# An LSTM's recurrent steps on one core: the weights as moving side, the state turned back each step

## The chip, the cores and the metric

The kernel runs on one core of a Trainium2 chip. The metric is the time of one execution in microseconds of device time. Three runs of the kernel before gave 6598.71, 6599.22 and 6603.01 us; the median is 6599.22.

## What is computed

Two layers on a batch of 64 graphs of 256 nodes with 256 features. The part that the change touches is the LSTM of the first layer, which reads the normalised output of the first graph stage:

```python
def _lstm(x, W_ih, W_hh, b_ih, b_hh):
    x_proj = jnp.einsum('btd,gd->btg', x, W_ih) + b_ih + b_hh
    ...
    def step(carry, xp):
        h, c = carry
        gates = xp + h @ W_hh.T
        i, f, g, o = jnp.split(gates, 4, axis=-1)
        c = jax.nn.sigmoid(f) * c + jax.nn.sigmoid(i) * jnp.tanh(g)
        h = jax.nn.sigmoid(o) * jnp.tanh(c)
        return ((h, c), h)
```

There are 64 sequences of 256 steps, 256 units and 4 x 256 gate values. Everything is float32. The rest (graph convolutions before and after, and a feed-forward layer with piecewise maxima) stays as it is.

## The kernel before

`full_kernel` runs six stages one after the other: `stage_gnn0`, `stage_lstm`, `stage_gnn1`, `stage_hinges`, `stage_tropical`, `stage_ffn`. All engines meet at a barrier between two stages. The tile `hx` [128, 2, 257, 64] lies in SBUF through the first three stages: partition and second index are the feature (or unit), the third is the step, the last is the sequence. `stage_gnn0` writes the inputs into places 1 to 256. `stage_lstm` reads the input of step t at place t+1 and later writes h of step t over it, so that `stage_gnn1` finds the states there.

In `stage_lstm` the gates lie with their units in the partitions and the sequences in the free dimension. Weights are the stationary side, 128x128 a call, and the state (128x64) or the input streams. One PSUM bank holds one gate of four steps (`ps_g[s][q]`, two sets s of four gates q). VectorE first writes the biases into a bank (`fill`, L505), then TensorE adds the input product of four steps at once (`input_part`, L567, 256 columns a call) and, step by step, the product of the state (L580, 64 columns a call, 16 calls a step). All matmuls are issued with `start=False`, onto the banks that were opened once at the start (L591). The gates are ordered g, i, f, o. In the steady state a step on TensorE is the state product of step t (L580) and the input product of one gate of the next group of four steps (L567); TensorE waits for `h_ready` before the first.

ScalarE takes tanh of g and sigmoid of i, f, o as each gate is done (L545), and tanh of c (L548). VectorE computes i*g (L512), c*f (L515), c (L518) and h (L521), which it writes straight into `hx`, and one fill a step (L505). GpSimd does nothing in this stage. Every engine runs the same steps; a semaphore count per step ties them together. Each float32 call of a matmul shows in the trace as two pairs of LDWEIGHTS (PEld) and MATMUL (PE), called passes below. A transpose is one pass.

Of the kernel before, what the change touches and what calls it, by code (L numbers as in the profile page):

```python
# [440 lines left out]
def stage_lstm(nc, a, hx):  # L441

    T, S = N, 4
    ROWS = GATES * H // P
    sems = []
    with ExitStack() as ctx:
# [34 lines left out]
        def _(sp):
            sp.dma_start(w_ih[:, :, :], a["w_ih_t"].rearrange("(k p) g -> p k g", p=P)).then_inc(const_in, 16)
            sp.dma_start(w_hh[:, :, :], a["w_hh_t"].rearrange("(k p) g -> p k g", p=P)).then_inc(const_in, 16)
            for e, name in enumerate(("b_ih", "b_hh")):
                sp.dma_start(bias[:, e, :, :], a[name].rearrange("m (q c) -> m q c", c=2)).then_inc(bias_in, 16)

        @block.vector
        def _(dve):  # L490
            dve.memset(hx[:, :, 0:1, :], 0.0).then_inc(zero_set, 1)
            dve.memset(c[:, :, :], 0.0).then_inc(zero_set, 1)
            dve.wait_ge(bias_in, 16 * 2)
            dve.tensor_tensor(bias_sum[:, :, :], bias[:, 0, :, :], bias[:, 1, :, :], ALU.add).then_inc(bias_ready, 1)
            dve.wait_ge(bias_ready, 1)
            for q in range(GATES):
                for c2 in range(2):
                    dve.tensor_copy(bias_wide[:, q, c2, :], bias_sum[:, q, c2:c2 + 1].to_broadcast([P, S * B]))\
                       .then_inc(bias_ready, 1)
            dve.wait_ge(bias_ready, 1 + 2 * GATES)  # L500
# [29 lines left out]
            for q in range(GATES):  # L530
                fill(0, q)
            groups(0)
            with dve.Fori(1, T // (2 * S)) as i:
                groups(i)

        @block.scalar
        def _(act):
            def step(t, s, r):
# [11 lines left out]
            def groups(i):  # L550
                for s in range(2):
                    for r in range(S):
                        step(2 * S * i + S * s + r, s, r)

            groups(0)
            with act.Fori(1, T // (2 * S)) as i:
                groups(i)

        @block.tensor
        def _(pe):  # L560
            def input_part(group, s, q):

                pe.wait_ge(bias_set, GATES * group + q + 1)
                for c2 in range(2):
                    row = (2 * q + c2) * P
                    for k in range(KD):
# [2178 lines left out]
```

## Time and profile before

| | |
|---|---|
| median of 3 runs | 6599.22 us |
| profiled execution | span 6600.3 us; no time beside its span is given for it |
| TensorE, matmul | 5873.0 us busy, 89% |
| TensorE, weight loads | 4098.8 us, 62% |
| VectorE | 5019.6 us, 76% |
| ScalarE | 3265.9 us, 49% |
| GpSimd | 1711.4 us, 26% |
| recurrent stage | from about 529 to 1915 us |

The spans are of one execution, counted from its first instruction. The shares are averages over six stages with different limits; the rows further down take the recurrent stage alone. PE is the matmul side of TensorE and PEld its weight loads, which run beside it; DVE is VectorE, ACT ScalarE, POOL GpSimd. Ends of matmuls are modelled in the trace, starts are measured.

### The profile page before, as it was taken

What the parts mean: (1) busy time and instruction counts of PE and PEld (TensorE: products, weight loads), DVE (VectorE), ACT (ScalarE), POOL (GpSimd) and SP (SyncE); (2) the same over time, 40 slices, a digit from 0 to 9 for tenths busy, and PEclk for the clock granted to TensorE, in tenths of its full rate; (3) what the DMA queues carried; (4) which work ended last, traced back from release to release, by engine and by line L of the source; (5) the groups of instructions that cost most, each with busy time, mean ns of one, the idle gap of its engine ahead of it and who ended that gap; (6) DMA issues with size and microseconds to landing.
All of it is one profiled execution on the core that took longest, in us unless ns stands there. A gap on an engine that the chain in (4) does not pass through costs nothing. (4 is left out here: it accounts for less than half of the span.)

```text
span 6600.3 us, 102260 instructions
## 1 busy us (share of the span) xinstructions
PE 5873.0 (89%) x29118; PEld 4098.8 (62%) x29118; DVE 5019.6 (76%) x9365; ACT 3265.9 (49%) x6025; POOL 1711.4 (26%) x3544
## 2 busy tenths in 40 slices
PE   9998999999988886399999999487676999999999
PEld 6667999999977775266666666354343444444444
DVE  8993333333348887799999999798686999999998
ACT  6662222222224443266666666121124777777777
POOL 3330000000004443266656655137561000000000
PEclk9999999999989998699999999799787999999999
DMA  4440000000014444122222222126453212222221
GB/s 135 135 137 21 0 0 0 0 0 0 0 45 153 153 153 141 60 72 72 73 75 72 72 75 73 33 101 217 160 203 109 83 64 83 77 74 72 83 83 45
DMA packets 359366, 528.00 MB, mean 80 GB/s; under 512 B 28208, under 2 KB 298160, under 8 KB 359248
## 3 DMA queue, kind: packets, MB, share of 16 engines
q1 hardware_dynamic: 322944, 400.58, 18.6%
q0 software_dynamic: 36304, 126.13, 5.6%
q8 instruction: 40, 0.66, 0.0%
q14 instruction: 78, 0.64, 0.0%
HBM read 297.48 MB, written 229.13 MB: 80 GB/s over the span
## 5 line engine op out<-in xcount | busy, mean ns | idle before, releaser
L1712 PE MATMUL t_fetched<-t_wpart,t_onehot 128*128 128x512 f32 x4096 | 1221.1, 420 | 36.1 <-DVE t_tout L1817 15.9
L1817 DVE SCALAR_TENSOR_TENSOR t_tout<-t_fetched,t_top,t_tout 128x1024 f32<-128x1024 f32 x896 | 1149.1, 1282 | 35.5 <-PE t_fetched L1712 4.5
L580 PEld LDWEIGHTS l_ps<-hx,l_whh 128*128 128x128 f32 x8192 | 962.5, 193 | 16.8 <-DVE hx L521 3.7
L580 PE MATMUL l_ps<-hx,l_whh 128*128 (+1 forms) x8192 | 950.5, 275 | 3.2 <-DVE hx L521 3.2
L1712 PEld LDWEIGHTS t_fetched<-t_wpart,t_onehot 128*128 128x128 f32 x4096 | 691.2, 188 | 269.0 <-DVE t_tout L1817 131.5
L545 ACT ACTIVATE l_act<-l_ps 128x128 f32<-128x128 f32 x1024 | 284.1, 278 | 1054.0 <-PE l_ps L580 1054.0
L2634 DVE SCALAR_TENSOR_TENSOR f_line<-f_hinge,f_vec,f_line 128x1024 f32<-128x1024 f32 x512 | 656.8, 1283 | 60.3 <-ACT f_hinge L2518 30.6
L2140 PE MATMUL ts_fetched<-t_wpart,ts_onehot 128*128 128x512 f32 x1608 | 509.5, 452 | 161.2 <-ACT ts_onehot L2115 71.3
L512 DVE TENSOR_TENSOR l_ig<-l_act 128x128 f32<-128x128 f32 x256 | 74.8, 292 | 592.1 <-ACT l_act L545 592.1
L2140 PEld LDWEIGHTS ts_fetched<-t_wpart,ts_onehot 128*128 128x128 f32 x1608 | 308.5, 209 | 309.9 <-DVE ts_tout L2208 196.2
L567 PE MATMUL l_ps<-hx,l_wih 128*128 (+1 forms) x2048 | 497.5, 386 | 1.0 <-DVE l_ps L505 1.0
L2555 PE MATMUL f_psc<-f_x,f_wc 128*128 128x512 f32 x1024 | 489.9, 601 | 0.0
L2568 PE MATMUL f_pso<-f_fused,f_wd 128*128 128x512 f32 x1024 | 463.0, 595 | 28.7 <-DVE f_fused L2621 28.7
L2555 PE MATMUL f_psg<-f_x,f_wg 128*128 128x512 f32 x1024 | 482.0, 593 | 0.0
L2112 ACT ACTIVATE ts_dist<-ts_index,t_pminus 128x256 f32<-128x256 f32 (+2 forms) x140 | 79.5, 568 | 655.0 <-PE ts_index L2131 544.6
L2518 ACT ACTIVATE f_hinge<-f_pst,f_vec 128x1024 f32<-128x1024 f32 x384 | 398.9, 1114 | 0.0
L567 PEld LDWEIGHTS l_ps<-hx,l_wih 128*128 128x128 f32 x2048 | 369.8, 190 | 41.5 <-issue 1.8
L2208 DVE SCALAR_TENSOR_TENSOR ts_tout<-ts_fetched,ts_top,ts_tout 128x1024 f32<-128x1024 f32 x296 | 380.0, 1284 | 13.4 <-PE ts_fetched L2140 3.0
L2568 PEld LDWEIGHTS f_pso<-f_fused,f_wd 128*128 128x128 f32 x1024 | 191.9, 190 | 283.6 <-issue 254.8
L775 POOL MEMSET g_half<- 128x2 f32 x1 | 0.1, 100 | 1395.5 <-POOLq L56 1395.5
L2555 PEld LDWEIGHTS f_psg<-f_x,f_wg 128*128 128x128 f32 x1024 | 195.6, 191 | 247.3 <-issue 247.3
L2525 ACT ACTIVATE f_spare<-f_pst,f_vec 128x1024 f32 x224 | 240.7, 1135 | 174.9 <-DVE f_pause L2659 174.9
(383 smaller groups left out, 10615.0 us busy)
## 6 DMA issues: line engine op xcount, KB each, us to landing
t<-t_tout SPq DMA_DIRECT2D x128, 512.0 KB, 2.6
f_t<-t SPq DMA_DIRECT2D x64, 1024.0 KB, 5.2
g_adj<-in_adj SPq DMA_DIRECT2D x128, 256.0 KB, 3.0
g_adjt<-in_adjt SPq DMA_DIRECT2D x128, 256.0 KB, 2.8
t_x<-x_normalised SPq DMA_DIRECT2D x130, 128.0 KB, 2.3
g_x<-in_x SPq DMA_DIRECT2D x64, 256.0 KB, 2.8
x_kept<-g_x SPq DMA_DIRECT2D x64, 256.0 KB, 2.2
g_x<-x_kept SPq DMA_DIRECT2D x64, 256.0 KB, 2.8
```

Source lines behind the costliest of these rows:

```text
L545: act.activation(act_g[q][:, :, :], ps_g[s][q][:, :, r, :], ACT.Tanh if q == 0 else ACT.Sigmoid)\
L567: pe.matmul(ps_g[s][q][:, c2, :, :], w_ih[:, k, row:row + P], hx[:, k, ds(S * group + 1, S), :], start=False, stop=False, skip_group_check ...
L580: mm = pe.matmul(ps_g[s][q][:, c2, r, :], w_hh[:, k, row:row + P], hx[:, k, ds(t, 1), :].rearrange("p o b -> p (o b)"), start=False, stop= ...
L1712: mm = pe.matmul(fetched[c % RING][:, h * CH:(h + 1) * CH], one_hot[g][:, c % GRP * P:(c % GRP + 1) * P], w_part[part][:, k, h * CH:(h + 1 ...
L1817: dve.scalar_tensor_tensor(t_out[j][:, :], column[:, :], value, t_out[j][:, :], ALU.add, ALU.max)\
L2140: mm = pe.matmul(fetched[buf][:, h * CH:(h + 1) * CH], one_hot[b][:, at * P:(at + 1) * P], w_part[part][:, half, h * CH:(h + 1) * CH], sta ...
L2208: dve.scalar_tensor_tensor(t_out[j][:, :], column[:, :], top[j][:, c:c + 1], (t_out if c else t_in)[j][:, :], ALU.add, ALU.max).then_inc(f ...
L2518: op = act.activation(hinge[v][:, k, :], ps_t[:, :], ACT.Relu, bias=column(u, "knot", k))
L2525: act.activation(spare[:, ds(k, 1), :].rearrange("p o t -> p (o t)"), ps_t[:, :], ACT.Relu, bias=column(u, "knot", k + SURE))
L2555: mm = pe.matmul(ps_[:, :], w_[:, k, u * P:(u + 1) * P], x[j][:, k, h * HB:(h + 1) * HB], start=(k == 0), stop=(k == KD - 1))
L2568: mm = pe.matmul(ps_o[k][:, h * HB:(h + 1) * HB], w_d[:, u, k * P:(k + 1) * P], fused[u % 2][:, h * HB:(h + 1) * HB], start=(u == 0), stop ...
L2634: dve.scalar_tensor_tensor(acc[:, :], source, column(u, "bend", k), acc[:, :], ALU.mult, ALU.add)\
```

## The change

The gates now lie with the sequences in the partitions: partitions 0 to 63 hold the 64 sequences for the first 128 units, 64 to 127 the same sequences for the other 128 units, and the free dimension holds the units of the gates. The stationary side of a matmul is the state or the input, [128, 64] (`h_t` or `x_now`), and the weights stream, 256 columns a call: one half of the units of two gates. The half c2 of the units is written at PSUM partitions 64*c2 and so uses columns 64*c2 to 64*c2+63 of the array. A pair p of gates (g and i, f and o) is done after 4 calls, both after 8 (L601). The input product is now made per step, one step ahead (8 calls), after the state product of the step. The bias fill is one copy of 512 elements a step as before.

h comes out of VectorE with the sequences in the partitions, so TensorE transposes it (L623, one call of 128x128 into `ps_ht`) and VectorE copies it from PSUM into one of two `h_t` tiles (L571), which is what the next step's state product waits for. GpSimd copies the state into `hx` (L531) and takes the next input out of `hx` into one of two `x_now` tiles (L522); before each copy it waits and does a one-element operation. The input product waits for `x_ready` and `bias_set`. ScalarE waits once for two gates. The banks are opened by 4 calls instead of 8. The loops are unrolled by 4 steps instead of 8. On the host the biases are laid out by halves.

```diff
-    T, S = N, 4
-    ROWS = GATES * H // P
+    T, U = N, 4
+    AHEAD = 1
+    HB = B
+    PAIRS = GATES // 2
...
-        w_ih = sb("l_wih", [P, KD, GATES * H])
-        w_hh = sb("l_whh", [P, KD, GATES * H])
-        bias = sb("l_bias", [P, 2, GATES, 2])
-        bias_sum = sb("l_bias_sum", [P, GATES, 2])
-        bias_wide = sb("l_bias_wide", [P, GATES, 2, S * B])
-        act_g = [sb(f"l_act{q}", [P, 2, B]) for q in range(GATES)]
-        c = sb("l_c", [P, 2, B])
-        ig = sb("l_ig", [P, 2, B])
-        tc_ = sb("l_tc", [P, 2, B])
-        ps_g = [[ctx.enter_context(nc.psum_tensor(f"l_ps{s}{q}", [P, 2, S, B], F32)) for q in range(GATES)]
-                for s in range(2)]
+        w_ih = sb("l_wih", [P, KD, GATES, 2, P])
+        w_hh = sb("l_whh", [P, KD, GATES, 2, P])
+        bias = sb("l_bias", [P, 2, GATES, P])
+        bias_sum = sb("l_bias_sum", [P, GATES, P])
+        act_g = [sb(f"l_act{q}", [P, P]) for q in range(GATES)]
+        c = sb("l_c", [P, P])
+        ig = sb("l_ig", [P, P])
+        tc_ = sb("l_tc", [P, P])
+        h = sb("l_h", [P, P])
+        ident = sb("l_ident", [P, P])
+        h_t = [sb(f"l_ht{j}", [P, KD, HB]) for j in range(2)]
+        x_now = [sb(f"l_x{j}", [P, KD, HB]) for j in range(2)]
+        pool_pause, pool_zero = sb("l_pool_pause", [1, 4]), sb("l_pool_zero", [1, 1])
+        ps_g = [ctx.enter_context(nc.psum_tensor(f"l_ps{j}", [P, PAIRS, 512], F32)) for j in range(2)]
+        ps_ht = ctx.enter_context(nc.psum_tensor("l_psht", [P, KD, HB], F32))
...
+        def groups(eng, step):
+            for r in range(U):
+                step(r, r)
+            with eng.Fori(1, T // U - 1) as i:
+                for r in range(U):
+                    step(U * i + r, r)
+            for r in range(U):
+                step(T - U + r, r)
...
+        @block.gpsimd
+        def _(pool):
+            def held(k, sem_, value):
+                pool.wait_ge(sem_, value)
+                pool.tensor_tensor(pool_pause[:, k:k + 1], pool_zero[:, :], pool_zero[:, :], ALU.add)
+            def take_x(t, j):
+                pool.tensor_copy(x_now[j][:, :, :], hx[:, :, ds(t + 1, 1), :].rearrange("p k o b -> p k (o b)"))\
+                    .then_inc(x_ready, 1)
+            def step(t, r):
+                if within(t, AHEAD + 1):
+                    held(r % 2, x_used, t + AHEAD)
+                    take_x(t + AHEAD + 1, (r + AHEAD + 1) % 2)
+                held(2 + r % 2, h_t_ready, t + 1)
+                pool.tensor_copy(hx[:, :, ds(t + 1, 1), :].rearrange("p k o b -> p k (o b)"), h_t[r % 2][:, :, :])\
+                    .then_inc(h_kept, 1)
+            pool.memset(pool_zero[:, :], 0.0).then_inc(pool_zero_set, 1)
+            pool.wait_ge(pool_zero_set, 1)
+            take_x(0, 0)
+            take_x(1, 1)
+            groups(pool, step)
...
-            def fill(s, q):
-                dve.tensor_copy(ps_g[s][q][:, :, :, :].rearrange("p c r b -> p c (r b)"), bias_wide[:, q, :, :])\
-                   .then_inc(bias_set, 1)
-            def step(t, s, r):
-                fill(1 - s, r)
+            def fill(r):
+                dve.tensor_copy(ps_g[r % 2][:, :, 0:2 * P], bias_sum[:, :, :].rearrange("p (o q) u -> p o (q u)", q=2))                   .then_inc(bias_set, 1)
+            def step(t, r):
+                if within(t, AHEAD):
+                    fill(r + AHEAD)
                 dve.wait_ge(act_ready[0], t + 1)
                 dve.wait_ge(act_ready[1], t + 1)
-                dve.tensor_tensor(ig[:, :, :], act_g[0][:, :, :], act_g[1][:, :, :], ALU.mult).then_inc(ig_ready, 1)
+                dve.tensor_tensor(ig[:, :], act_g[0][:, :], act_g[1][:, :], ALU.mult).then_inc(ig_ready, 1)
                 dve.wait_ge(act_ready[2], t + 1)
                 wait_past(dve, c_ready, t)
-                dve.tensor_tensor(c[:, :, :], c[:, :, :], act_g[2][:, :, :], ALU.mult).then_inc(fc_ready, 1)
+                dve.tensor_tensor(c[:, :], c[:, :], act_g[2][:, :], ALU.mult).then_inc(fc_ready, 1)
                 dve.wait_ge(ig_ready, t + 1)
                 dve.wait_ge(fc_ready, t + 1)
-                dve.tensor_tensor(c[:, :, :], c[:, :, :], ig[:, :, :], ALU.add).then_inc(c_ready, 1)
+                dve.tensor_tensor(c[:, :], c[:, :], ig[:, :], ALU.add).then_inc(c_ready, 1)
                 dve.wait_ge(act_ready[3], t + 1)
                 dve.wait_ge(tanh_c_ready, t + 1)
-                dve.tensor_tensor(hx[:, :, ds(t + 1, 1), :].rearrange("p k o b -> p k (o b)"), act_g[3][:, :, :],
-                                  tc_[:, :, :], ALU.mult).then_inc(h_ready, 1)
-            def groups(i):
-                for s in range(2):
-                    for r in range(S):
-                        step(2 * S * i + S * s + r, s, r)
+                dve.tensor_tensor(h[:, :], act_g[3][:, :], tc_[:, :], ALU.mult).then_inc(h_ready, 1)
+                dve.wait_ge(h_turned, t + 1)
+                wait_past(dve, h_kept, t - 1)
+                dve.tensor_copy(h_t[r % 2][:, :, :], ps_ht[:, :, :]).then_inc(h_t_ready, 1)
...
+            def step(t, r):
                 for q in range(GATES):
-                    act.wait_ge(gate_done[q], t + 1)
-                    if q == 0:
-                        wait_past(act, h_ready, t)
-                    act.activation(act_g[q][:, :, :], ps_g[s][q][:, :, r, :], ACT.Tanh if q == 0 else ACT.Sigmoid)\
+                    if q % 2 == 0:
+                        act.wait_ge(pair_done[q // 2], t + 1)
+                    act.activation(act_g[q][:, :], ps_g[r % 2][:, q // 2, (q % 2) * P:(q % 2 + 1) * P], ACT.Tanh if q == 0 else ACT.Sigmoid)\
                        .then_inc(act_ready[q], 1)
                 act.wait_ge(c_ready, t + 1)
-                act.activation(tc_[:, :, :], c[:, :, :], ACT.Tanh).then_inc(tanh_c_ready, 1)
...
+            def half(j, c2, p):
+                return ps_g[j][c2 * HB:(c2 + 1) * HB, p, 0:2 * P].rearrange("b (q u) -> b q u", u=P)
+            def products(p, j, source, w, last):
+                for k in range(KD):
+                    for c2 in range(2):
+                        mm = pe.matmul(half(j, c2, p), source[:, k, :], w[:, k, 2 * p:2 * p + 2, c2, :],
+                                       start=False, stop=last and k == KD - 1, skip_group_check=True)
+                return mm
+            def input_part(t, j):
+                pe.wait_ge(x_ready, t + 1)
+                pe.wait_ge(bias_set, t + 1)
+                for p in range(PAIRS):
+                    mm = products(p, j, x_now[j], w_ih, False)
+                mm.then_inc(x_used, 1)
+            def step(t, r):
+                wait_past(pe, h_t_ready, t)
+                for p in range(PAIRS):
+                    products(p, r % 2, h_t[(r + 1) % 2], w_hh, True).then_inc(pair_done[p], 1)
+                if within(t, AHEAD):
+                    input_part(t + AHEAD, (r + AHEAD) % 2)
+                pe.wait_ge(h_ready, t + 1)
+                pe.transpose(ps_ht[:, :, :].rearrange("p k b -> p (k b)"), h[:, :], ident[:, :]).then_inc(h_turned, 1)
+            pe.wait_ge(const_in, 16 * 3)
+            for j in range(2):
+                for p in range(PAIRS):
+                    mm = pe.matmul(ps_g[j][:, p, :], ident[:, :], w_ih[:, 0, :, 0, :], start=True, stop=True)
             mm.then_inc(banks_opened, 1)
             pe.wait_ge(zero_set, 2)
-            for q in range(GATES):
-                input_part(0, 0, q)
-            for s in range(2):
-                steps(0, s, False)
-            with pe.Fori(1, T // (2 * S) - 1) as i:
-                for s in range(2):
-                    steps(i, s, False)
-            for s in range(2):
-                steps(T // (2 * S) - 1, s, s == 1)
+            for r in range(AHEAD):
+                input_part(r, r)
+            groups(pe, step)
```

TensorE, in the loop, one step before (`l_ps00` is set 0, gate 0; L580 is the state product, L567 the input product, counts are calls):

```order
L580 MATMUL l_ps00<-hx,l_whh 128x64 [waits l_h_ready]
L580 MATMUL l_ps00<-hx,l_whh 128x64 x3
L580 MATMUL l_ps01<-hx,l_whh 128x64 x4
L580 MATMUL l_ps02<-hx,l_whh 128x64 x4
L580 MATMUL l_ps03<-hx,l_whh 128x64 x4
L567 MATMUL l_ps13<-hx,l_wih 128x256 [waits l_bias_set]
L567 MATMUL l_ps13<-hx,l_wih 128x256 x3
```

The same engine and place now (`l_ht` is the turned state, `l_x` the input, `l_psht` the transpose of h):

```order
L601 MATMUL l_ps1<-l_whh,l_ht0 64x256 [waits l_h_t_ready]
L601 MATMUL l_ps1<-l_whh,l_ht0 64x256 x7
L607 REGISTER_ALU
L601 MATMUL l_ps0<-l_wih,l_x0 64x256 [waits l_bias_set,l_x_ready]
L601 MATMUL l_ps0<-l_wih,l_x0 64x256 x7
L623 MATMUL l_psht<-l_ident,l_h 128x128 [waits l_h_ready]
```

The 16 calls on 128x128 weights and 4 of the input product have become 8 and 8 with a 128x64 stationary side, and a step ends with a transpose that waits for h; the next state product waits for the copy of it.

VectorE in the loop, one step before (L505 is the fill, L521 writes h):

```order
L510 REGISTER_ALU
L512 TENSOR_TENSOR l_ig<-l_act0,l_act1 128x128 [waits l_act_ready1,l_act_ready0]
L515 TENSOR_TENSOR l_c<-l_c,l_act2 128x128 [waits l_c_ready,l_act_ready2]
L518 TENSOR_TENSOR l_c<-l_c,l_ig 128x128 [waits l_fc_ready,l_ig_ready]
L521 ISA [waits l_tanh_c_ready,l_act_ready3]
L521 TENSOR_TENSOR hx<-l_act3,l_tc 128x2x64
L505 COPY l_ps03<-l_bias_wide 128x512
```

VectorE now (L551 is the fill, L567 writes h, L571 copies the transpose):

```order
L556 REGISTER_ALU
L558 TENSOR_TENSOR l_ig<-l_act0,l_act1 128x128 [waits l_act_ready1,l_act_ready0]
L561 TENSOR_TENSOR l_c<-l_c,l_act2 128x128 [waits l_c_ready,l_act_ready2]
L564 TENSOR_TENSOR l_c<-l_c,l_ig 128x128 [waits l_fc_ready,l_ig_ready]
L567 TENSOR_TENSOR l_h<-l_act3,l_tc 128x128 [waits l_tanh_c_ready,l_act_ready3]
L571 COPY l_ht0<-l_psht 128x128 [waits l_h_kept,l_h_turned]
L551 COPY l_ps0<-l_bias_sum 128x2x256
```

The register instruction ahead of h is gone and a copy out of PSUM that waits for `h_turned` and `h_kept` has come in; the fill of the next step stands behind it.

GpSimd now, one step of the loop; it had no instruction here before:

```order
L518 TENSOR_TENSOR l_pool_pause<-l_pool_zero 1x1 [waits l_x_used]
L522 ISA
L522 COPY l_x1<-hx 128x128
L518 TENSOR_TENSOR l_pool_pause<-l_pool_zero 1x1 [waits l_h_t_ready]
L531 ISA
L531 COPY hx<-l_ht1 128x2x64
L518 TENSOR_TENSOR l_pool_pause<-l_pool_zero 1x1 [waits l_x_used]
```

The copy of an input and the copy of a state alternate, each behind a wait and a pause of one element.

## Rows read from the trace of the kernel before

**Rows 1.** Windows: us, then busy us and count of PE, PEld, DVE, ACT, POOL, granted clock.
```profile
552.00:1915.00 1363.00, 1358.83 (x10211) 1306.08 (x10209) 455.62 (x1279) 336.31 (x1281) 0.00 (x0) 0.99 0.00 0
...
1899.00:1907.00 8.00, 6.93 (x33) 6.74 (x33) 1.61 (x6) 1.31 (x5) 0.00 (x0) 0.50 0.01 2
```

**Rows 2.** Waits from 600 to 1900 us: who waited for whom, total, times, longest.
```profile
ACT l_act L545 <- PE l_ps L580: 978.7, 980, 2.1
...
PE l_ps L580 <- DVE hx L521: 2.1, 2, 1.1
```

**Rows 3.** Timeline of one step in the loop: start us, duration us, engine, line, operation.
```profile
1400.31 3.68 PE L580 MATMUL l_ps<-hx,l_whh 128*128 x32
...
1403.13 0.28 ACT L545 ACTIVATE l_act<-l_ps 128x128 f32<-128x128 f32 x1 [0.62 <-PE l_ps L580]
1403.44 0.29 DVE L515 TENSOR_TENSOR l_c<-l_c,l_act 128x128 f32<-128x128 f32 x1 [0.53 <-ACT l_act L545]
...
1403.82 1.95 PE L567 MATMUL l_ps<-hx,l_wih 128*128 x8
1403.84 0.29 DVE L518 TENSOR_TENSOR l_c<-l_c,l_ig 128x128 f32<-128x128 f32 x1
1404.02 0.28 ACT L545 ACTIVATE l_act<-l_ps 128x128 f32<-128x128 f32 x1 [0.62 <-PE l_ps L580]
1404.20 0.30 ACT L548 ACTIVATE l_tc<-l_c 128x128 f32<-128x128 f32 x1
1404.71 0.29 DVE L521 TENSOR_TENSOR hx<-l_act,l_tc 128x128 f32 x1 [0.58 <-ACT l_tc L548]
...
1405.61 0.33 PE L580 MATMUL l_ps<-hx,l_whh 128*128 x2
```

**Rows 4.** Timeline of a step outside the loop.
```profile
561.50 0.30 ACT L548 ACTIVATE l_tc<-l_c 128x128 f32<-128x128 f32 x1
561.90 0.29 DVE L521 TENSOR_TENSOR hx<-l_act,l_tc 128x128 f32<-128x128 f32 x1 [0.47 <-ACT l_tc L548]
```

**Rows 5.** Timeline of the stage's start: the banks opened, the first input product; durations min/median/max.
```profile
534.66 9.68 PE L591 MATMUL l_ps<-hx,l_wih 128*128 128x512 f32 x16 [11.54 <-DMA l_whh<-in_w_hh_t]
...
542.46 0.19 PEld L591 LDWEIGHTS l_ps<-hx,l_wih 128*128 128x128 f32 x1 [0.24 <-issue]
...
545.33 7.14 PE L567 MATMUL l_ps<-hx,l_wih 128*128 128x256 f32 x32 [0.98 <-DVE l_ps L505]
...
L580 PEld LDWEIGHTS l_ps<-hx,l_whh x8192: 186/192/338, 552.1 to 1913.5; 128*128 128x128 f32 x200
...
L567 PE MATMUL l_ps<-hx,l_wih x2048: 379/379/454, 545.3 to 1887.7; 128*128 x175, 128*128 128x256 f32 x12
```

**Rows 6.** Timeline of the last steps, without an input product.
```profile
1887.91 3.68 PE L580 MATMUL l_ps<-hx,l_whh 128*128 128x64 f32 x32
...
1888.94 0.28 ACT L545 ACTIVATE l_act<-l_ps 128x128 f32<-128x128 f32 x1 [2.14 <-PE l_ps L580]
...
1892.65 5.06 PE L580 MATMUL l_ps<-hx,l_whh 128*128 128x64 f32 x32 [1.07 <-DVE hx L521]
1893.80 0.28 ACT L545 ACTIVATE l_act<-l_ps 128x128 f32<-128x128 f32 x1 [1.70 <-PE l_ps L580]
...
1914.75 0.29 DVE L521 TENSOR_TENSOR hx<-l_act,l_tc 128x128 f32 x1 [1.39 <-ACT l_tc L548]
```

**Rows 7.** Timeline of the next stage: four transposes in a stream, and four after a wait.
```profile
2209.67 0.60 PE L875 MATMUL g_ps_xn3t<-g_ident,g_xn 128*128 128x128 f32 x4
...
2209.69 0.99 DVE L964 TENSOR_SCALAR g_xn<-g_x,g_mv,g_rstd 128x256 f32<-128x256 f32 x2 [0.86 <-POOL g_rstd L788]
...
2210.74 0.66 PE L875 MATMUL g_ps_t<-g_ident,g_xn 128*128 128x128 f32 x4 [0.47 <-DVE g_xn L964]
```

**Rows 8.** GpSimd's groups of this size: count, busy us, mean ns.
```profile
L1615 POOL TENSOR_TENSOR t_poolpause<-t_logshare 1x1 f32<-1x1 f32 x384 | 70.3, 183 | 513.2 <-DVE t_done L1826 510.4 <-DVE t_cand L1805 2.8
L793 POOL TENSOR_TENSOR g_adjt<-g_adjt,g_ident 128x128 f32<-128x128 f32 x128 | 58.8, 480 | 0.0
```

More of the change, by code:

```diff
@@ L482, in _, with within @@
+        def within(t, ahead):
+            return not isinstance(t, int) or t + ahead < T
         @block.sync
         def _(sp):
-            sp.dma_start(w_ih[:, :, :], a["w_ih_t"].rearrange("(k p) g -> p k g", p=P)).then_inc(const_in, 16)
-            sp.dma_start(w_hh[:, :, :], a["w_hh_t"].rearrange("(k p) g -> p k g", p=P)).then_inc(const_in, 16)
+            for w, name in ((w_ih, "w_ih_t"), (w_hh, "w_hh_t")):
+                sp.dma_start(w[:, :, :, :, :].rearrange("p k q c u -> p k (q c u)"),
+                             a[name].rearrange("(k p) g -> p k g", p=P)).then_inc(const_in, 16)
+            sp.dma_start(ident[:, :], a["ident"]).then_inc(const_in, 16)
@@ L489, in _ @@
         @block.vector
         def _(dve):
-            dve.memset(hx[:, :, 0:1, :], 0.0).then_inc(zero_set, 1)
-            dve.memset(c[:, :, :], 0.0).then_inc(zero_set, 1)
-            dve.wait_ge(bias_in, 16 * 2)
+            dve.memset(h_t[1][:, :, :], 0.0).then_inc(zero_set, 1)
+            dve.memset(c[:, :], 0.0).then_inc(zero_set, 1)
+            dve.wait_ge(bias_in, 16 * 4)
             dve.tensor_tensor(bias_sum[:, :, :], bias[:, 0, :, :], bias[:, 1, :, :], ALU.add).then_inc(bias_ready, 1)
@@ L495, in _ @@
             dve.wait_ge(bias_ready, 1)
-            for q in range(GATES):
[L497 to L500, printed above, removed]
-            dve.wait_ge(zero_set, 2)
-            def fill(s, q):
-                dve.tensor_copy(ps_g[s][q][:, :, :, :].rearrange("p c r b -> p c (r b)"), bias_wide[:, q, :, :])\
-                   .then_inc(bias_set, 1)
@@ L530, in _ @@
[L530 to L534, printed above, removed]
+                dve.tensor_tensor(h[:, :], act_g[3][:, :], tc_[:, :], ALU.mult).then_inc(h_ready, 1)
+                dve.wait_ge(h_turned, t + 1)
+                wait_past(dve, h_kept, t - 1)
+                dve.tensor_copy(h_t[r % 2][:, :, :], ps_ht[:, :, :]).then_inc(h_t_ready, 1)
+            dve.wait_ge(banks_opened, 1)
+            for r in range(AHEAD):
+                fill(r)
@@ L546, in step @@
                        .then_inc(act_ready[q], 1)
                 act.wait_ge(c_ready, t + 1)
-                act.activation(tc_[:, :, :], c[:, :, :], ACT.Tanh).then_inc(tanh_c_ready, 1)
-            def groups(i):
-                for s in range(2):
[L552 to L557, printed above, removed]
+                act.activation(tc_[:, :], c[:, :], ACT.Tanh).then_inc(tanh_c_ready, 1)
@@ L559, in _ @@
+            groups(act, step)
         @block.tensor
         def _(pe):
[L561 to L566, printed above, removed]
-                        pe.matmul(ps_g[s][q][:, c2, :, :], w_ih[:, k, row:row + P],
-                                  hx[:, k, ds(S * group + 1, S), :], start=False, stop=False,
-                                  skip_group_check=True)
@@ L571, in steps @@
-            def steps(i, s, last):
-                group = 2 * i + s
-                for r in range(S):
-                    t = S * group + r
-                    wait_past(pe, h_ready, t)
-                    for q in range(GATES):
-                        for c2 in range(2):
-                            row = (2 * q + c2) * P
-                            for k in range(KD):
-                                mm = pe.matmul(ps_g[s][q][:, c2, r, :], w_hh[:, k, row:row + P],
-                                               hx[:, k, ds(t, 1), :].rearrange("p o b -> p (o b)"), start=False,
-                                               stop=(r == S - 1 and c2 == 1 and k == KD - 1), skip_group_check=True)
-                        mm.then_inc(gate_done[q], 1)
-                    if not last:
-                        input_part(group + 1, 1 - s, r)
@@ L588, in _ @@
-            pe.wait_ge(const_in, 16 * 2)
-            for s in range(2):
-                for q in range(GATES):
-                    mm = pe.matmul(ps_g[s][q][:, :, :, :], w_ih[:, 0, 0:P], hx[:, 0, ds(1, 2 * S), :], start=True, stop=True)
+            def half(j, c2, p):
+                return ps_g[j][c2 * HB:(c2 + 1) * HB, p, 0:2 * P].rearrange("b (q u) -> b q u", u=P)
+            def products(p, j, source, w, last):
+                for k in range(KD):
+                    for c2 in range(2):
+                        mm = pe.matmul(half(j, c2, p), source[:, k, :], w[:, k, 2 * p:2 * p + 2, c2, :],
+                                       start=False, stop=last and k == KD - 1, skip_group_check=True)
+                return mm
@@ L601, in _ @@
-            for s in range(2):
-                steps(T // (2 * S) - 1, s, s == 1)
+            for r in range(AHEAD):
+                input_part(r, r)
+            groups(pe, step)
     clear_semaphores(nc, sems)
@@ L2706, in columns, with by_half @@
         return np.ascontiguousarray(v.reshape(-1, P).T)
+    def by_half(v):
+        return np.ascontiguousarray(v.reshape(GATES, 2, P).transpose(1, 0, 2).reshape(2, -1))
     ones = np.ones((P, P), np.float32)
@@ L2715 @@
         "w_hh_t": turned(gates_first_g(given["L0_ffn_W_hh"])),
-        "b_ih": columns(gates_first_g(given["L0_ffn_b_ih"])), "b_hh": columns(gates_first_g(given["L0_ffn_b_hh"])),
+        "b_ih": by_half(gates_first_g(given["L0_ffn_b_ih"])), "b_hh": by_half(gates_first_g(given["L0_ffn_b_hh"])),
         "w_lin_t": turned(given["L0_ffn_W_lin"]), "b_lin": given["L0_ffn_b_lin"].reshape(1, 2),
```

14 lines of the change are left out of this document (7 added, 7 removed).

## The prediction

> **What bounds the kernel now.** I read the windows by stage first: of 6600.3 us the recurrent stage (552 to 1915) holds 1363, and in it TensorE is busy for 1358.8 while VectorE has 456, ScalarE 336 and GpSimd nothing [rows 1]. The waits say the same from the other side: 980 waits of ScalarE for TensorE, and only two of TensorE for the new state [rows 2]. The timeline of one step shows why. A step begins with 32 passes of the state's product (two per call, 16 calls), 3.51 us from 1400.31 to 1403.82, then 8 passes of the input's product, 1.79 us; the next step's first pass is at 1405.61, so a step is 5.30 us of TensorE alone [rows 3]. The state was ready at 1405.00, 0.6 us before it could be used. In the product of the state each pass streams only 64 columns but loads 128x128 weights, and costs 0.110 us; a pass of 256 columns costs (7.14 - 0.38) / 31 = 0.218 us [rows 5]. So the loads of weights set the pace in two thirds of the step, and that is what the change goes for.
>
> **The change, part by part.**
>
> *The products.* State and input become the stationary side (128x64) and the weights stream, 256 columns at a time. Each product is now 8 calls, 16 passes: 4 pairs, one call of each pair for each half of the array's columns. One behind the other they are 16 x 0.218 = 3.49 us. If a pass on one half runs beside a pass on the other, the order of the calls (both passes of one half, both of the other) lets the second pass of each call run beside the first of the next: 9 slots of 0.218 where a product stands alone, 1.96 us; both products of a step behind each other take 17 slots, 3.71 us, instead of 5.30. No row of this kernel has a stationary side of 64 columns, so the trace bounds it from both sides: 3.71 and 32 x 0.218 = 6.98 us. I take 3.71: the passes use different cells and write different partitions, and the rows show that TensorE already does two things at once, loads of 0.192 us beside passes that follow each other every 0.110 us [rows 3, 5]. The Trainium skill (TensorEngine Tiling (Array Packing), Key Properties) says that different tiles can execute loads and matmuls in parallel; no run here shows it. By it the step's products are the 3.71, without it the 6.98.
>
> *The chain.* With that TensorE no longer covers the chain of one step, so it has to be added up. From the first pass of the state's product: the last starts 8 slots later, 1.74; it takes 0.38 [rows 5]; 0.03 to ScalarE, and the sigmoid of f is 0.28; 0.03 and 0.29 for c*f; 0.11 and 0.29 for the add; 0.07 and 0.30 for the tanh [rows 3]; 0.10 and 0.29 for h, the distance that the steps outside the loop show (561.80 to 561.90) [rows 4]. In the loop it is 0.21 because the address of hx goes through a register, which now falls to GpSimd. That is 3.91. New behind it: TensorE takes up work 0.06 after the write it waits for (2210.68 to 2210.74); one transpose from idle is 0.33, by the four that take 0.66 after a wait and start 0.11 apart [rows 7]; 0.10 (two waits) and 0.29 for VectorE's copy out of PSUM, by its other operations of this size; 0.06 to TensorE, and 0.12 for a first pass whose weights could not be loaded ahead: after a wait the first activation came 1.15 us after the first pass (1892.65 to 1893.80), else 1.03 (1887.91 to 1888.94) [rows 6]. Sum: **4.87 us** against 5.30.
>
> *Does TensorE keep up?* 3.71 of products and 0.16 until the last has left the array end at 3.87, just before the transpose can start at 3.97. If TensorE sets the end instead, the step is 3.71 + 0.16 + 0.33 + 0.10 + 0.29 + 0.06 + 0.12 = 4.77. The two are 0.10 apart: whatever lengthens the products by more than that is paid in full. The switch between half and full tiles twice a step has no row. Its bounds are 0 and one emptying of the array, 0.16; I take 0, since the array is empty at both switches by this sum. The Trainium skill (same page and section) asks that the engine be drained at such a switch; by it nothing changes while these waits stand.
>
> *GpSimd* gets two pauses (0.18) and two copies of 128x128 a step (0.48 for a two-input operation of this size) [rows 8]: 1.3 us of 4.87. Its copy of the input is due one product of the state later, its copy of h two steps later; neither ends last. VectorE has 5 operations of 0.29 and the fill of 0.69: 2.1 us, and the fill lies under the state's product.
>
> *Ends.* Opening the banks takes 8 passes of 512 instead of 16: 3.4 us less at 0.43 (0.19 and 0.24) a pass [rows 5]. The first input product takes 1.74 instead of 6.98. So the first step starts 8.6 us sooner. Before, the steps run from 552.31 (545.33 + 6.98) to the end of the last h at 1915.04, 1362.7 us [rows 5, 6]; now 255 x 4.87 + 5.4 (copy and last write by GpSimd) = 1247.3. Together 115.4 + 8.6 = **124 us less**. The page gives the profiled execution by its span, 6600.3, which is 1.1 us above the median of the three runs, 6599.2; taken from the median it gives **6475**. Every 0.01 us a step is 2.6 us; the step that changes nothing is 5.35.
>
> **Rivals.**
> - *Loads of the second half come late* (slower). This is the mechanism that decides the sign. While one pass runs on each half, the next weights for half A stand in the queue behind a pass for half B that has to wait. If they can't be taken past it, each call starts later by one load of 64 columns, half of the 0.110 that a load of 128 costs where loads set the pace [rows 3]: 0.055. A step's TensorE bound becomes 4.77 + 16 x 0.055 = 5.65, and the time 6475 + 256 x 0.78 = 6675. It decides from 0.036 us a call. For it: this interleaving of half tiles appears nowhere in the trace. Against it: loads do run beside passes on full tiles. The Trainium skill (TensorE: Matmul & The Clock Gate, Part 3, The mechanism) says that a load overlaps a running matmul only when the rows of the array differ; both halves here use all rows, so by that rule this rival, or worse, holds. The rows of the state's product disagree for full tiles.
> - *The halves don't run side by side*: the change does not do what it says. 6.98 + 1.06 = 8.04 us a step, 7286 us. Nothing in the trace excludes it.
> - *The clock falls.* The granted clock was 0.99 over the stage and 0.50 (1.2 of 2.4 GHz) in its last steps, when the input's product was gone and TensorE waited 1.07 us a step for the state [rows 1, 6]. Passes then took twice as long. The new step has gaps too (0.1 and 0.5 us). If it fell for good, 3.71, 0.16 and 0.33 double: 4.77 + 4.20 = 8.97 us, 7525. Against it: the gaps are half as long and the products fill three quarters of the step.
>
> **How the numbers follow.** Forecast 0.47, with its own range of 6431 (0.17 less a step: 0.03 instead of 0.07 before the tanh and 0.10 before the copy, half the 0.12) to 6544 (0.11 more for register waits, 0.16 for a switch). Late loads 0.33, of which 0.08 below the deciding 0.036. Serial halves 0.14, low clock 0.06. The predicted time is the first case's. The range takes in the first two, 0.80: 6430 to 6700, the top at 0.061 us a call. A measurement of this kernel tells 0.2%, 13 us, from no change. Faster 0.47 + 0.08 = 0.55, same 0.04 (steps of 5.30 to 5.40), slower 0.41.
>
> **What would show it.** Right: h to h of 4.8 to 5.0 us; passes of L601 starting in near pairs, 16 of them in about 2 us; TensorE waiting for h before each transpose and for h_t before each state product; clock 1.00. Late loads: starts of the calls 0.25 or more apart, and the transpose starting when the input's product ends while h is long there. Serial: 16 passes in 3.5 us. Wrong in the chain: a tail from the last pass to the first of the next step other than 2.75 us. Stages before and after should keep their lengths.

## The result, and the profile after

The changed kernel takes **6392.94 us** (median of four runs, 6392.48 to 6393.44) against 6599.88 us of the kernel before beside it (6598.71 to 6603.01): ratio 0.9684, 95% interval 0.967 to 0.9698, 207 us less. The forecast was 6475, range 6430 to 6700. The sign is as forecast, and so is what was to bring it, the two halves side by side; the time is 37 us below the range.

The stage by windows (us, then busy us and count of PE, PEld, DVE, ACT, POOL, granted clock), the answer to [rows 1]:

```profile
552.00:1700.00 1148.00, 1015.00 (x8367) 595.29 (x8367) 528.94 (x1524) 304.96 (x1270) 199.80 (x1012) 1.00 0.00 0
1690.00:1700.00 10.00, 6.77 (x53) 3.68 (x51) 4.03 (x13) 2.40 (x10) 0.82 (x4) 1.00 0.00 0
```

TensorE is no longer busy all the time (1015 of 1148 us, before 1358.8 of 1363), and its clock stays at 1.00, that is 2.4 GHz, in the last steps too, where it was 0.50 before. The waits from 600 to 1900 us (total, times, longest) answer to [rows 2]:

```profile
ACT l_act L584 <- PE l_ps L601: 664.2, 487, 2.4
...
PEld l_ps L601 <- DVE l_ht L571: 144.8, 243, 0.7
...
PEld l_psht L623 <- DVE l_h L567: 139.3, 244, 2.3
```

Two waits of the product for the state have become one a step, and the transpose has its own: the chain of the step now sets the pace. One step in the loop, and the copy of the step ahead (start, duration), the answer to [rows 3]:

```profile
999.54 0.29 DVE L571 COPY l_ht<-l_psht 128x128 f32<-128x128 f32 x1 [0.51 <-PE l_psht L623]
...
1004.04 0.29 DVE L571 COPY l_ht<-l_psht 128x128 f32<-128x128 f32 x1 [0.42 <-PE l_psht L623]
...
1004.38 1.49 PEld L601 LDWEIGHTS l_ps<-l_whh,l_ht 128*64 128x64 f32 x16 [0.57 <-DVE l_ht L571]
1004.38 1.95 PE L601 MATMUL l_ps<-l_whh,l_ht 128*64 128x256 f32 x16 [0.38 <-DVE l_ht L571]
...
1005.51 0.45 ACT L584 ACTIVATE l_act<-l_ps 128x128 f32<-128x128 f32 x2 [2.29 <-PE l_ps L601]
...
1006.16 1.90 PE L601 MATMUL l_ps<-l_wih,l_x 128*64 128x256 f32 x16
1006.38 0.45 ACT L584 ACTIVATE l_act<-l_ps 128x128 f32<-128x128 f32 x2 [0.42 <-PE l_ps L601]
1006.69 0.29 DVE L561 TENSOR_TENSOR l_c<-l_c,l_act 128x128 f32<-128x128 f32 x1 [0.33 <-ACT l_act L584]
1007.08 0.29 DVE L564 TENSOR_TENSOR l_c<-l_c,l_ig 128x128 f32<-128x128 f32 x1
1007.41 0.31 ACT L587 ACTIVATE l_tc<-l_c 128x128 f32<-128x128 f32 x1 [0.58 <-DVE l_c L564]
1007.82 0.29 DVE L567 TENSOR_TENSOR l_h<-l_act,l_tc 128x128 f32<-128x128 f32 x1 [0.44 <-ACT l_tc L587]
...
1008.17 0.33 PE L623 MATMUL l_psht<-l_ident,l_h 128*128 128x128 f32 x1
1008.53 0.29 DVE L571 COPY l_ht<-l_psht 128x128 f32<-128x128 f32 x1 [0.42 <-PE l_psht L623]
...
1008.88 0.63 PEld L601 LDWEIGHTS l_ps<-l_whh,l_ht 128*64 128x64 f32 x8 [0.57 <-DVE l_ht L571]
```

From the first pass at 1004.38 to the next step's at 1008.88 it is 4.50 us. The input's product begins 1.78 after the state's, so 16 passes take 8 slots. The transpose starts 0.35 after h, the copy 0.36 later, the next product 0.35 after that; from tanh to h it is 0.41, against 0.40 in [rows 4]. The sigmoid of f stands in the second ACT row of two operations (1006.38), 2.00 after the first pass. Of the steps in the loop, which is unrolled by four, every fourth is 0.09 longer: VectorE's copy comes 0.45 after the transpose's start and not 0.36 (it stood for 0.51 us at 999.54, for 0.42 at 1004.04); in that step VectorE has a register instruction of 0.04 us ahead of the copy (999.46), for the count of `h_kept`, which itself waits for the transpose; in the others it has none there. The mean over the stage is 4.517 us, from GpSimd's first copy of a state (548.3) to its last (1700.1), 255 steps. The start of the stage answers to the timeline in [rows 5]:

```profile
534.28 5.64 PE L628 MATMUL l_ps<-l_wih,l_ident 128*128 128x512 f32 x8 [12.01 <-DMA l_ident<-in_ident]
...
540.90 1.95 PE L601 MATMUL l_ps<-l_wih,l_x 128*64 128x256 f32 x16 [0.98 <-DVE l_ps L551]
...
542.65 1.93 PE L601 MATMUL l_ps<-l_whh,l_ht 128*64 128x256 f32 x16
```

The groups (count, busy us, mean ns, idle before) and durations of single tiles (min/median/max ns) answer to the durations in [rows 5] and to [rows 7, 8]:

```profile
L601 PE MATMUL l_ps<-l_whh,l_ht 128*64 128x256 f32 x4096 | 498.5, 385 | 103.2 <-DVE l_ht L571 103.2
...
L531 POOL COPY hx<-l_ht 128x128 f32 (+1 forms) x256 | 71.6, 280 | 0.0
```

```profile
L623 PE MATMUL l_psht<-l_ident,l_h x256: 327/328/329, 547.4 to 1699.3; 128*128 128x128 f32 x128
L571 DVE COPY l_ht<-l_psht x256: 291/292/292, 547.8 to 1699.6; 128x128 f32<-128x128 f32 x128
```

GpSimd's copies take 280 ns, not the 480 of the two-input operation that stood in for them, and end long before anyone needs them.

### The profile page after: what moved, and what is told of

Its sections match the earlier page's. It is cut to its first block and busy times, and to the rows that moved or that the text cites. A ratio compares the mean times of both kernels' runs of the same rounds, so it can differ in the third digit from the quotient of the medians.

```text
span 6390.7 us, 100252 instructions
## 1 busy us (share of the span) xinstructions
PE 5520.0 (86%) x27318; PEld 3377.2 (53%) x27318; DVE 5095.3 (80%) x9609; ACT 3238.1 (51%) x6025; POOL 1914.4 (30%) x4567
## 5 line engine op out<-in xcount | busy, mean ns | idle before, releaser
L584 ACT ACTIVATE l_act<-l_ps 128x128 f32<-128x128 f32 x1024 | 228.2, 275 | 716.9 <-PE l_ps L601 716.9
L601 PE MATMUL l_ps<-l_whh,l_ht 128*64 128x256 f32 x4096 | 498.5, 385 | 103.2 <-DVE l_ht L571 103.2
L601 PE MATMUL l_ps<-l_wih,l_x 128*64 128x256 f32 x4096 | 485.6, 379 | 1.0 <-DVE l_ps L551 1.0
L601 PEld LDWEIGHTS l_ps<-l_whh,l_ht 128*64 128x64 f32 x4096 | 271.7, 136 | 262.6 <-DVE l_ht L571 151.9
L518 POOL TENSOR_TENSOR l_pool_pause<-l_pool_zero 1x1 f32<-1x1 f32 x510 | 93.8, 184 | 972.0 <-DVE l_ht L571 956.1
L601 PEld LDWEIGHTS l_ps<-l_wih,l_x 128*64 128x64 f32 x4096 | 294.7, 137 | 148.9 <-issue 1.8
L2665 DVE SCALAR_TENSOR_TENSOR f_line<-f_spare,f_vec,f_line 128x1024 f32<-128x1024 f32 x224 | 287.8, 1285 | 44.2 <-DVE f_line L2665 44.2
```

The source lines that it names most:

```text
L518: pool.tensor_tensor(pool_pause[:, k:k + 1], pool_zero[:, :], pool_zero[:, :], ALU.add)
L584: act.activation(act_g[q][:, :], ps_g[r % 2][:, q // 2, (q % 2) * P:(q % 2 + 1) * P], ACT.Tanh if q == 0 else ACT.Sigmoid)\
L601: mm = pe.matmul(half(j, c2, p), source[:, k, :], w[:, k, 2 * p:2 * p + 2, c2, :], start=False, stop=last and k == KD - 1, skip_group_chec ...
L2665: dve.scalar_tensor_tensor(acc[:, :], source, column(u, "bend", k), acc[:, :], ALU.mult, ALU.add)\
```

## The experiments

The steps are means: from the first to the last copy of a state by GpSimd, over 255, and for the kernel before 1362.7 / 256.

| | us | ratio to before, 95% | step, us |
|---|---|---|---|
| before | 6599.88 | | 5.32 |
| changed | 6392.94 | 0.9684 [0.967, 0.9698] | 4.517 |
| e1_one_half | 7235.24 | 1.096 [1.0928, 1.0991] | 7.778 |
| e2_halves_grouped | 6400.23 | 0.9695 [0.9667, 0.9723] | 4.556 |
| e3_not_turned | 7289.25 | 1.1041 [1.1009, 1.1074] | 3.794 |
| e4_input_one_call | 6527.62 | 0.9888 [0.9859, 0.9916] | 5.332 |
| e5_f_before_o | 6354.96 | 0.9621 [0.9605, 0.9637] | 4.358 |
| e6_split_and_late | 6289.27 | 0.952 [0.9504, 0.9536] | 4.100 |

The kernel before took 6600.51 beside e1 to e4 and 6606.54 beside e5 and e6.

### e1: all calls on one half of the array

```diff
-                return ps_g[j][c2 * HB:(c2 + 1) * HB, p, 0:2 * P].rearrange("b (q u) -> b q u", u=P)
+                return ps_g[j][0:HB, p, 0:2 * P].rearrange("b (q u) -> b q u", u=P)
```

> All calls of both products write to partitions 0 to 63, so none has a neighbour on the other half of the array; the gates of the other 64 partitions are left out (they keep the bias). Theory A, passes on the two halves run side by side: without a neighbour the 32 passes of a step come every 0.215 us, 6.9 us, and with 0.33 for the transpose, 0.04 + 0.29 for the copy and 0.05 + 0.05 to the next product a step is 7.6 to 7.8 us instead of 4.49, about 7200 us. Theory B, a pass with a stationary side of 64 columns is by itself twice as fast, whichever half it is on: passes every 0.107 us as before, a step of 4.49, 6393 us.

Measured 7235.24, a step of 7.78. From its timeline:

```profile
1000.88 0.29 DVE L567 TENSOR_TENSOR l_h<-l_act,l_tc 128x128 f32<-128x128 f32 x1 [0.45 <-ACT l_tc L587]
...
1002.78 0.33 PE L623 MATMUL l_psht<-l_ident,l_h 128*128 128x128 f32 x1
...
1003.49 3.67 PE L601 MATMUL l_ps<-l_whh,l_ht 128*64 128x256 f32 x16 [0.38 <-DVE l_ht L571]
...
1007.00 2.32 PE L601 MATMUL l_ps<-l_wih,l_x 128*64 128x256 f32 x10
```

The state's 16 passes take 3.51 us until the input's begin (1003.49 to 1007.00), almost twice the 1.78 of the changed kernel, and the transpose stands 1.9 us behind h, until the products are through. The streams, loads and counts are the same in both; only the place in the array differs. So the two halves do run side by side, and it is this that carries the change: with streamed weights alone a step would be 2.46 us longer than before. The Trainium skill (TensorEngine Tiling (Array Packing), Key Properties) says that tiles load and multiply in parallel; this run agrees for the matmuls, at a factor of 3.51 / 1.78 = 1.97.

### e2: each half's four passes one behind the other

```diff
-                for k in range(KD):
-                    for c2 in range(2):
+                for c2 in range(2):
+                    for k in range(KD):
```

> The same calls, those of one half of the units behind one another (both k of half 0, then both k of half 1, for each pair of gates). Theory A with strict order: in each group of four passes three have no neighbour, 25 slots of 0.215 for the two products instead of 16, 5.4 us, a step of about 6.1 us, 6800 us. Theory A where a pass may start ahead of others that wait for the other half, four or more ahead: nothing changes, 4.49 and 6393 us. Theory B: nothing changes either.

Measured 6400.23, 7 us more than the changed kernel (the intervals of the two ratios overlap) and 0.04 a step by the traces. In program order four passes of one half now come ahead of the first of the other. If passes started in that order, each group of four would share only one slot with the next, 13 slots or 2.8 us a product. Windows of 0.02 to 0.03 us of PE at the product's start show how many passes run (the count in brackets), first e2, then the changed kernel, then e1:

```profile
1002.30:1002.32 0.02, 0.02 (x2) 1.00 0.00 0
```

```profile
1004.38:1004.40 0.02, 0.02 (x2) 1.00 0.00 0
```

```profile
1003.49:1003.52 0.03, 0.03 (x1) 1.00 0.00 0
```

Two passes run from the first moment where there are two halves, even where the second half's first pass is the fifth in the queue, and one where there is one half. A pass that waits for its half does not hold back passes of the other. That is the reason why a product takes 8 slots and not 9. Late loads do show in this run, at a small price: for the second pair of gates the load of the second half starts only with the first half's pass (1003.22), and from the next passes on the two halves start 0.06 apart (1003.43 and 1003.49) instead of 0.01. The 0.04 a step can come from there; nothing was tried on it. The Trainium skill (TensorE: Matmul & The Clock Gate, Part 3, The mechanism) lets a load run beside a matmul only if their rows differ; both halves here use all rows, and their loads are hidden all the same (16 loads between 1004.38 and 1005.87, under passes with a pair every 0.215 us), so the measurement decides.

### e3: the state not turned back

```diff
-                dve.tensor_tensor(h[:, :], act_g[3][:, :], tc_[:, :], ALU.mult).then_inc(h_ready, 1)
-                dve.wait_ge(h_turned, t + 1)
                 wait_past(dve, h_kept, t - 1)
-                dve.tensor_copy(h_t[r % 2][:, :, :], ps_ht[:, :, :]).then_inc(h_t_ready, 1)
+                dve.tensor_tensor(h_t[r % 2][:, :, :].rearrange("p k b -> p (k b)"), act_g[3][:, :], tc_[:, :], ALU.mult)\
+                   .then_inc(h_t_ready, 1)
...
-                pe.wait_ge(h_ready, t + 1)
-                pe.transpose(ps_ht[:, :, :].rearrange("p k b -> p (k b)"), h[:, :], ident[:, :]).then_inc(h_turned, 1)
```

> The turning back of the state is left out: VectorE writes h as it lies into the tile that the next product reads, without transpose and copy (so the recurrence is another one). If the chain through h sets the step, the 0.37 of the transpose and 0.34 of the copy go: 4.49 - 0.71 = 3.78 us a step, 182 us less, about 6211 us. If TensorE's own work set the step (32 passes, 3.44, plus 0.05), the gain would end at about 3.5 to 3.8 as well, so it is told by whether the product waits for the state. Rival: the step is set by something else (GpSimd's copies), then little changes.

The step is 3.794 us, 0.72 less. The total, 7289.25, says nothing of that: the stages with piecewise maxima do work that depends on the values they get, and these are others here. The groups of lines show far more of a loop (`tg_fetched`, 2048 passes) that takes 64 passes in the changed kernel, and more rounds of another (1736 passes against 1608):

```profile
L2322 PE MATMUL tg_fetched<-t_wpart,tg_runrows 128*128 128x512 f32 x2048 | 678.7, 483 | 403.0 <-DVE tg_runrows L2339 264.5 <-DVE tg_acc L2356 138.5
...
L2167 PE MATMUL ts_fetched<-t_wpart,ts_onehot 128*128 128x512 f32 x1736 | 544.0, 446 | 175.1 <-DVE ts_tout L2235 76.4 <-ACT ts_onehot L2142 61.8 <-issue 20.3
```

So of this run only the recurrent stage is read. Turning costs the chain what the timeline of the changed kernel shows, 0.35 and 0.36 us; 0.01 is left. A price of the switch between half and full tiles would stand inside these links and the next: the transpose starts 0.06 after h ends and the product 0.06 after the copy ends, and here, where the array never leaves its halves, the product starts 0.05 after h ends (1004.44 + 0.29 to 1004.78). So a switch of an idle array costs 0.01 at most. TensorE did both products of a step every 3.79 us here.

### e4: seven of eight calls of the input product left out

```diff
-                for p in range(PAIRS):
-                    mm = products(p, j, x_now[j], w_ih, False)
+                mm = pe.matmul(half(j, 1, 0), x_now[j][:, 0, :], w_ih[:, 0, 0:2, 1, :],
+                               start=False, stop=False, skip_group_check=True)
```

> Of the input product of each step one call of eight is left; seven are left out. Theory A of the cover: the input product lies wholly under the chain, so a step stays at 4.49 and the time at 6393 as long as the clock stays. The clock is the question: before, it fell in the last steps when the input product was gone. If it falls here too, the state product doubles to 3.4 and the transpose slows, 4.49 + 1.56 + 0.3 = 6.3 to 6.6 us a step, 6860 to 6930 us. I expect the fall.

The step is 5.33 us, *longer* than with the input product. The data of later stages differ here too (1464 passes of the same loop), so the step counts. The clock over the stage, and two products of the state:

```profile
600.00:1900.00 1300.00, 899.03 (x4626) 455.80 (x4628) 506.83 (x1460) 291.54 (x1215) 191.63 (x972) 0.78 0.00 0
```

```profile
999.58 1.95 PE L601 MATMUL l_ps<-l_whh,l_ht 128*64 128x256 f32 x16 [0.38 <-DVE l_ht L571]
...
1003.37 0.33 PE L623 MATMUL l_psht<-l_ident,l_h 128*128 128x128 f32 x1 [1.41 <-DVE l_h L567]
...
1004.08 3.56 PE L601 MATMUL l_ps<-l_whh,l_ht 128*64 128x256 f32 x16 [0.38 <-DVE l_ht L571]
...
1009.47 0.33 PE L623 MATMUL l_psht<-l_ident,l_h 128*128 128x128 f32 x1 [1.33 <-DVE l_h L567]
```

The first product runs at 2.4 GHz (1.95 us) and its step is 4.50 (999.58 to 1004.08), just that of the changed kernel: the input product costs the chain nothing. The next takes 3.56 us for the same 16 passes, at 1.2 GHz, and from transpose to transpose it is 6.10 us. The clock did not stay down, as I had expected, but went in and out, 0.78 on the mean. What TensorE did otherwise is in the rows: it stood idle for 1.3 to 1.4 us before each transpose, where in the changed kernel the input product ran. So the input product, free by itself, also keeps the clock up; less work for TensorE made a longer step.

### e5: f ahead of o

Each set of gates gets three banks (g and i; f; o), filled by two copies instead of one, and f and o are made by calls of 128 columns, so that f is done before o.

```diff
+            def products(p, j, source, w, last, qs=(0, 1)):
+                lo, n = qs[0], len(qs)
+                if p == 1 and n == 2:
+                    products(1, j, source, w, last, (0,))
+                    return products(1, j, source, w, last, (1,))
...
-                for p in range(PAIRS):
-                    products(p, r % 2, h_t[(r + 1) % 2], w_hh, True).then_inc(pair_done[p], 1)
+                products(0, r % 2, h_t[(r + 1) % 2], w_hh, True).then_inc(pair_done[0], 1)
+                products(1, r % 2, h_t[(r + 1) % 2], w_hh, True, (0,)).then_inc(pair_done[1], 1)
+                products(1, r % 2, h_t[(r + 1) % 2], w_hh, True, (1,)).then_inc(o_done, 1)
```

> f and o are no pair any more: f is computed by calls of 128 columns ahead of o, each in a bank of its own (three banks a set), in both products; the fill is two copies; nothing is left out. Theory S, a pass costs what its columns stream: a call of 128 columns half a slot (0.107), so f is done 0.43 us sooner. The chain would be 4.06 us, but TensorE's own work (3.44 for both products, then 0.05, 0.06, 0.37, 0.34 and the copy's wait) holds a step at 4.2 to 4.35: 6330 to 6355 us. Theory L, weight loads set a floor of 0.107 us a pass: 48 passes are 5.1 us, a step 5.9 us, 6750 us.

Measured 6354.96, a step of 4.358. One step of it:

```profile
1002.27 1.72 PEld L605 LDWEIGHTS l_ps<-l_whh,l_ht 128*64 128x64 f32 x24 [0.66 <-DVE l_ht L573]
1002.28 1.96 PE L605 MATMUL l_ps<-l_whh,l_ht 128*64 128x256 f32 x24 [0.47 <-DVE l_ht L573]
...
1003.41 0.71 ACT L588 ACTIVATE l_act<-l_ps 128x128 f32<-128x128 f32 x3 [2.64 <-PE l_ps L605]
...
1004.06 1.91 PE L605 MATMUL l_ps<-l_wih,l_x 128*64 128x256 f32 x24
1004.16 0.28 DVE L563 TENSOR_TENSOR l_c<-l_c,l_act 128x128 f32<-128x128 f32 x1
...
1005.29 0.29 DVE L569 TENSOR_TENSOR l_h<-l_act,l_tc 128x128 f32<-128x128 f32 x1 [0.45 <-ACT l_tc L591]
...
1005.90 0.33 PE L629 MATMUL l_psht<-l_ident,l_h 128*128 128x128 f32 x1
...
1006.61 1.96 PE L605 MATMUL l_ps<-l_whh,l_ht 128*64 128x256 f32 x24 [0.39 <-DVE l_ht L573]
```

24 passes, 8 of them of 256 columns and 16 of 128, take 1.78 us (1002.28 to 1004.06), as 16 of 256 did: on halves a pass of 128 columns costs half of one of 256, and the loads set no floor at twice their rate. c*f starts 1.88 after the first pass instead of 2.31. But the transpose comes 0.61 after h and not 0.35: now the input product ends last, and more than half of what f gave is paid there. 0.10 of it comes with the change to a full tile behind running passes: the last pair of the input product starts at 1005.69 and the transpose 0.21 later, where pairs of 128 columns follow each other every 0.11; its load starts only there too (1005.90), so the two are not told apart. (0.43 less 0.26 is 0.17; the mean step fell by 0.16.)

### e6: and the last quarter of the input product behind the transpose

```diff
                 pe.transpose(ps_ht[:, :, :].rearrange("p k b -> p (k b)"), h[:, :], ident[:, :]).then_inc(h_turned, 1)
+                if within(t, AHEAD):
+                    input_rest((r + AHEAD) % 2)
```

On top of e5: `input_part` makes g, i and f, and `input_rest` makes o.

> As e5_f_before_o, and the last quarter of the input product (that of o) is issued behind the transpose, where TensorE waits for the copy. Theory S: TensorE no longer holds the transpose up, and the chain alone sets the step: 4.49 - 0.43 = 4.06 us, 110 us less than the changed kernel, 6283 us. Theory L: 5.3 us a step, 6600 us.

Measured 6289.27 (6286.12 to 6291.99), a step of 4.100. Its ratio to the kernel before, 0.952, lies clear of the changed kernel's 0.9684: it beats both, by 317 us and, with the difference of the ratios, 108 us. The place that mattered:

```profile
1005.29 0.29 DVE L569 TENSOR_TENSOR l_h<-l_act,l_tc 128x128 f32<-128x128 f32 x1 [0.45 <-ACT l_tc L591]
...
1005.64 0.33 PE L634 MATMUL l_psht<-l_ident,l_h 128*128 128x128 f32 x1
...
1005.90 0.66 PE L605 MATMUL l_ps<-l_wih,l_x 128*64 128x128 f32 x8
1006.01 0.29 DVE L573 COPY l_ht<-l_psht 128x128 f32<-128x128 f32 x1 [0.42 <-PE l_psht L634]
...
1006.39 1.92 PE L605 MATMUL l_ps<-l_whh,l_ht 128*64 128x256 f32 x24
```

The transpose is back at 0.35 behind h, and o's passes fill the time of VectorE's copy (1005.90 to the next product at 1006.39), which costs 0.03 at that end: 0.38 from copy to product instead of 0.35. The first of them starts 0.26 after the transpose, where full-tile transposes follow each other every 0.11 [rows 7]: a switch behind a running pass is not free here either, but the copy covers it.

## Why the forecast was right in kind and wrong in size

**The step.** I had 4.87 us; it is 4.50 in most steps and 4.517 on the mean. 255 x 0.353 is 90 us, somewhat more than the whole miss of the span, 86 (forecast 6600.3 - 124.0 = 6476.3, measured 6390.7). By my own terms:

| term | forecast | measured |
|---|---|---|
| first pass to the last | 8 slots, 1.74 | 1.78 less one slot of 0.22: 1.56 |
| first pass whose weights are not there | 0.12 more | in the 1.56 |
| last pass, and to the sigmoid of f | 0.38 + 0.03 | 0.44 |
| f to c*f, to the add | 0.31, 0.40 | 0.31, 0.39 |
| add to tanh | 0.29 + 0.07 | 0.33 |
| tanh to h | 0.30 + 0.10 | 0.41 |
| h to transpose | 0.29 + 0.06 | 0.35 |
| transpose to copy | 0.33 + 0.10 | 0.36 |
| copy to product | 0.29 + 0.06 | 0.35 |
| sum | 4.87 | 4.50 |

- *The step of the forecast that failed* is the first: "9 slots of 0.218 where a product stands alone", with the last pass 8 slots after the first, and 0.12 for weights "that could not be loaded ahead". It held passes to their order in the program. The halves fill at once (two passes in the first 0.02 us; e2), so the last pair starts after 7 slots. The 0.12 was misread from [rows 6]. In the step at 1892.65, after a wait, the second pass comes 0.160 after the first and the others 0.112 apart, so the first costs 0.05 more; the step at 1887.91, which I compared it with, is itself short at its start, its second pass comes 0.055 after the first. Here the second pair comes 0.267 after the first instead of 0.216, 0.05 again. Slot and misreading together are 0.30 of the 0.37 between 4.87 and 4.50.
- *The links* to the tanh and to the copy were 0.03 and 0.07 shorter than I took them; for the copy I had put "two waits" at 0.10, and the 0.07 ahead of the tanh was read in a step where ScalarE was still at the sigmoid of o (1404.02 + 0.28, the tanh at 1404.20) [rows 3]. Both lay in my low end. They count 256 times: 26 us.
- My low end, 6431, allowed 0.17 less a step, with half of the 0.12 in it but no slot: the order of the passes, which I had assumed and no row showed, should have been bounded from both sides as the other unknowns were.
- *TensorE's own bound* of 4.77 was too high as well: in e5, where the input product ends last, a step is 4.33 us (1002.28 to 1006.61).
- *The signs named.* h to h of 4.8 to 5.0 us: it was 4.50. 16 passes in about 2 us, in near pairs: 1.78, in pairs. TensorE waiting for h and for h_t, clock 1.00: so it was. A tail other than 2.75 us was to mean that the chain was wrong: from the end of the last pass (1005.94 + 0.38) to 1008.88 it is 2.56, the 0.12 and the 0.07 less.

**Ends.** The banks took 8 passes as forecast, and the first step starts 9.7 us sooner (552.31 to 542.65), against 8.6. The steps end 6.0 us after 255 mean steps, against 5.4. So the stage, from 542.65 to 1700.41, is 1157.8 us against my 1247.3 and 1362.7 before.

**Later stages** should have kept their lengths. From the last state to the end of the span it was 4685.3 us before (6600.3 - 1915.0) and 4690.3 after (6390.7 - 1700.4); it is 4690.0 in e2 and 4691.9 in e6. So 5 to 7 us more are spent there in these traces of the change. Of the kernel before there is this one trace, and its runs spread over 4.3 us (6598.71 to 6603.01), so part of it can be that. Some 2 of them lie between the last two piecewise stages, from the last `t_tout` to the first `ts_y` (79.2 us before, 81.5 after). Nothing was tried on this, and its cause is open. With it the account of the span closes: the stage took 89.5 less than forecast and began 1.1 sooner, 5.0 were lost, which is 85.6 below 6476.3, and the span is 6390.7.

**The rivals.** *Late loads of the second half* (6675) is out for this order of calls: pairs come every 0.215 us from the first to the last, loads between them, and for f and o e5 ran twice as many loads a column; e2's order had some, for 0.04 a step at most. *Halves one behind the other* (7286) is what e1 built by hand; it came to 7235, so the rival's price was right within 1%, and it did not happen. *The clock falls* (7525) did not happen in the changed kernel, whose clock was 1.00; e4 shows that it can, where TensorE is given less to do. GpSimd at 0.92 us a step instead of 1.3, and VectorE's fill, cost nothing, as said; e3's step of 3.79 had both in it.

## What to carry to other kernels

Where a small batch makes TensorE load more weights than it streams columns, turn the roles round only if the narrow stationary side can be split over two column tiles: here the same streams on one half were 2.46 us a step slower than before, on two halves 0.80 faster. Once a recurrent step is bound by its chain, look at which result the chain waits for and make it sooner (here f ahead of o), and put work that nobody waits for behind the transpose and not ahead of it; the first gave 0.16 us a step here, the second on top of it 0.26. Work taken from TensorE that nothing waited for can cost time by the clock, so read the granted clock with the step.

## What was not expected of the hardware

- Passes on the two halves start together although the program names them one half after the other, even with four passes of one half ahead (e2: two running in the first 0.02 us, and 0.04 us a step lost).
- A pass of 128 columns on a half tile takes half of one of 256 (24 passes in 1.78 us), with 24 loads of 137 ns in the same time. In the changed kernel's trace too the loads of a pair start 0.01 us or less apart, 137 ns each, so by the records loads on the two halves run side by side as well.
- With less to do, TensorE was granted less: a clock of 0.78 instead of 1.00 and a step of 5.33 us instead of 4.52, with seven eighths of one product gone (e4). The clock changed between neighbouring steps of the same program.
